# A recurrent block with a routed mixture of experts: x loads first, logits three chunks ahead, routing in smaller steps, dispatches in one row

## What is computed

```python
xn = _layernorm(x)
# s: a gated recurrence along each sequence
hidden, gate = split(xn @ W_hg)            # 256 columns each
a = sigmoid(-gate);  v = sigmoid(gate) * (relu(hidden) + 0.5)
h[t] = a[t] * h[t-1] + v[t];   s = h @ W_out
# ffn: one shared expert, and the best 2 of 16 experts by softmax(xn @ Wr)
shared = silu(xn @ Sg) * (xn @ Su) @ Sd
routed = sum over the 2 experts e:  p_e * (silu(xn @ Wg[e]) * (xn @ Wu[e]) @ Wd[e])
out = x + s * silu(routed + shared)
```

## Time and profile before

| | us |
|---|---|
| median of 3 runs (467.46, 472.47, 469.41) | 469.41 |
| profiled execution, its own time | 466.69 |
| its span (first to last instruction) | 464.5 |
| first phase, to ACT's last copy of it | 216.4 |
| PE idle for the dispatches of group 0 | 216.4 to 246.5 |
| second phase, first `gate_up` to last | 248.64 to 439.08 |
| PE / DVE / ACT / POOL busy | 324.3 / 257.2 / 243.9 / 184.8 |

### The profile page before, as it was taken

How to read it: one execution, slowest core, us unless ns; L and a number is a source line. 1 busy time by engine, 2 the same in 40 slices (tenths; PEclk the granted TensorE clock), 3 DMA queues, 4 the chain that set the end, 5 groups by cost and what they waited for, 6 DMA issues and landing times. The chain is left out here.

```text
span 464.5 us, 6051 instructions
## 1 busy us (share of the span) xinstructions
PE 324.3 (70%) x1532; PEld 206.5 (44%) x1532; DVE 257.2 (55%) x692; ACT 243.9 (53%) x518; POOL 184.8 (40%) x206
## 2 busy tenths in 40 slices
PE   0735999998957878894006644739889899989930
PEld 0423566655634445563003423515555555555520
DVE  3105587887885496797002740616656566666640
ACT  1552787688875447774004421526666566666520
POOL 4803111111111107636650477555445455555571
PEclk9985999999988789998556887779999999999985
DMA  4299999300000003452338135153444444444200
GB/s 142 85 331 418 412 414 377 165 2 1 1 1 0 1 0 133 176 223 100 128 140 276 65 130 206 65 156 102 126 133 138 139 139 137 121 118 119 71 3 0
DMA packets 27982, 63.81 MB, mean 137 GB/s; under 512 B 3701, under 2 KB 22784, under 8 KB 27056
## 3 DMA queue, kind: packets, MB, share of 16 engines
q1 hardware_dynamic: 20880, 45.78, 28.6%
q0 software_dynamic: 6784, 17.06, 9.9%
q10 hardware_dynamic: 288, 0.60, 0.4%
HBM read 29.52 MB, written 35.21 MB: 139 GB/s over the span
## 5 line engine op out<-in xcount | busy, mean ns | idle before, releaser
L318 POOL DMA_INDIRECT out<-arena x84 | 87.2, 1038 | 75.9 <-DVE arena L787 59.5
L899 PE MATMUL p_u<-xT,w_front 128*128 128x512 f32 x192 | 100.3, 659 | 2.1 <-DVE prod L526 2.0
L312 POOL DMA_INDIRECT slots<-arena,pos x64 | 65.6, 1024 | 65.2 <-issue 37.9
L763 DVE TENSOR_TENSOR arena<-p_u,arena 128x512 f32<-128x512 f32 x42 | 29.0, 691 | 109.0 <-ACT arena L423 93.7
L972 PE MATMUL p_u<-arena 128*128 x168 | 84.0, 624 | 0.0
L997 PEld LDWEIGHTS p_s<-arena 128*128 128x128 f32 x336 | 43.1, 198 | 53.7 <-issue 53.7
L997 PE MATMUL p_s<-arena 128*128 x336 | 49.5, 292 | 22.6 <-ACT arena L429 9.1
L409 ACT ACTIVATE arena<-arena 128x128 f32<-128x128 f32 x84 | 36.6, 483 | 51.0 <-DMA arena<-slots 50.8
L899 PEld LDWEIGHTS p_u<-xT,w_front 128*128 128x128 f32 x192 | 37.7, 212 | 37.3 <-issue 37.3
L276 POOL TENSOR_TENSOR var_eps<-meanvar,eps 128x4 f32<-128x4 f32 x16 | 3.5, 221 | 127.4 <-DVE meanvar L492 127.4
L948 PE MATMUL p_xt<-ident,arena 128*128 128x128 f32 x84 | 18.2, 301 | 46.6 <-ACT arena L409 45.3
(11 more groups left out here) (124 smaller groups left out, 468.5 us busy)
## 6 DMA issues: line engine op xcount, KB each, us to landing
slots<-arena SPq DMA_DIRECT2D x4, 4116.0 KB, 19.7
arena<-slots SPq DMA_DIRECT2D x42, 392.0 KB
arena<-in_W_lines SPq DMA_DIRECT2D x2, 2688.0 KB, 12.5
arena<-in_x SPq DMA_DIRECT2D x16, 256.0 KB, 14.4
arena<-in_W_lines SPq DMA_DIRECT2D x1, 2304.0 KB, 9.2
out<-arena POOLq DMA_INDIRECT x84
slots<-arena,pos POOLq DMA_INDIRECT x64
w_front<-in_W_front ACTq DMA_DIRECT2D x1, 392.0 KB, 3.6
```

The costliest lines, as they stand in the source:

```text
L312: pool.indirect_dma_start(slots, index, xrow[:, t], None).then_inc(signal, 16)
L318: pool.indirect_dma_start(out, index, xg[:, n % RX, h, X], None, bounds_check=T - 1, oob_is_err=False)\
L763: nc.vector.tensor_tensor(hg[:, :, :], p_u[:, n % 2 * 2:n % 2 * 2 + 2, 2 * P:4 * P], sil[:, n % 2], ALU.mult)\
L899: nc.tensor.matmul(p_u[:, n % 4], w_front[:, UPS[q]:UPS[q] + P], xT[:, c % XB], start=True, stop=True)\
```

## The change

- **x first.** SP issues all 16 chunks of x, then waits for the blank rows and issues the four fills.
- **Three ahead.** A table `READ` replaces `LEAD`: chunks 1, 2 in round 0; 3 in round 1; 4, 5 in round 2; i + 3 after that. `xT` gets four buffers, the statistics three. On PE the transposes stay between `up` 1 and 2, and the logits go from the middle of the round to its end; chunk 0's go behind its first two `up`. ACT's wait for all constants before the first normalisation is gone.
- **Routing spread.** Keys are made once per group (rounds 8 and 14). Group 0: counts in round 8, bases and first half in 9, second half in 10, probabilities in 9. Group 1: all in rounds 13 to 15. Each step stands at the start of DVE's round, ahead of `ln_stats` and the scans. The weights are split: DVE makes probabilities, POOL multiplies and adds (`block_weights`).
- **Dispatches.** POOL waits per half for positions and per chunk for `s_she`; no wait for its own dispatches; no store between group 1's dispatches.
- **Twelve slot buffers.** `RX` = 12; to make room, `sil`, `hg`, `hw`, `hT` of the second phase move onto the recurrence's buffers, free after the scans.

```diff
-XB = 3
-RX = 8
+XB = 4
+RX = 12
...
+        READ = {0: [1, 2], 1: [3], 2: [4, 5]} | {i: [i + 3] for i in range(3, NCH - 3)}
...
             for c in range(NCH):
                 load_x(c)
-                if c == 3:
-                    sp.wait_ge(s_blank, 2)
-                if c >= 3 and c % 3 == 0 and c < 15:
-                    q = c // 3 - 1
-                    rows = slots[q * SLOTS * P // 4:(q + 1) * SLOTS * P // 4]
-                    sp.dma_start(rows.rearrange("(p n) w -> p (n w)", p=P), arena[:, 0:SLOTS // 4 * ROW]).then_inc(s_init, 16)
+            sp.wait_ge(s_blank, 2)
+            for q in range(4):
+                rows = slots[q * SLOTS * P // 4:(q + 1) * SLOTS * P // 4]
+                sp.dma_start(rows.rearrange("(p n) w -> p (n w)", p=P), arena[:, 0:SLOTS // 4 * ROW]).then_inc(s_init, 16)
...
+            def block_weights(g):
...
+                pool.wait_ge(s_p01, g + 1)
+                weights = p01[:, :, a:b].rearrange("p k (t w) -> p k t w", w=1).to_broadcast([P, 2, n, BLOCK])
+                nc.gpsimd.tensor_tensor(eq4[:, :, 0:n], eq4[:, :, 0:n], weights, ALU.mult).then_inc(s_spot, 1)
+                pool.wait_ge(s_spot, g + 1)
+                nc.gpsimd.tensor_tensor(xrow[:, a:b, W4:W4 + BLOCK], eq4[:, 0, 0:n], eq4[:, 1, 0:n], ALU.add).then_inc(s_w4, 1)
+
+            for c in range(3, NCH):
                 rstd_of(c)
+            block_weights(0)
+            pool.wait_ge(s_w4, 1)
             pool.wait_ge(s_init, 64)
-            pool.wait_ge(s_w4, 1)
-            pool.wait_ge(s_pos, len(HALVES[0]))
-            pool.wait_ge(s_she, CHUNKS[0].stop)
             for t in TILES[0]:
-                if t > 0 and t % 8 == 0:
-                    pool.wait_ge(s_disp[0], 16 * min(t, FIRST_TILES))
-                    if t > FIRST_TILES:
-                        pool.wait_ge(s_disp[1], 16 * (t - FIRST_TILES))
+                if t == HALVES[0][0][0]:
+                    pool.wait_ge(s_pos, 1)
+                if t == HALVES[0][1][0]:
+                    pool.wait_ge(s_pos, 2)
+                if t % TT == 0:
+                    pool.wait_ge(s_she, t // TT + 1)
                 dispatch(s_disp[0] if t < FIRST_TILES else s_disp[1], t)
+            block_weights(1)
             pool.wait_ge(s_w4, 2)
-            pool.wait_ge(s_pos, len(HALVES[0]) + len(HALVES[1]))
-            pool.wait_ge(s_she, NCH)
-            early = [10, 14, 18]
-            for k, t in enumerate(TILES[1]):
-                if k in early:
-                    store_out(early.index(k))
+            pool.wait_ge(s_pos, 3)
+            for t in TILES[1]:
+                if t % TT == 0:
+                    pool.wait_ge(s_she, t // TT + 1)
                 dispatch(s_disp[2], t)
-            for n in range(len(early), PAIRS):
+            for n in range(PAIRS):
                 store_out(n)
...
+                if i == 7:
+                    route_top(2)
                     route_second(2)
                     shift_logits(0)
+                if i == 8:
+                    route_keys(0)
+                    count_keys(0)
+                if i == 9:
+                    key_bases(0)
+                    positions(0, 0)
+                if i == 10:
+                    positions(0, 1)
                 if i == 11:
                     tile_keys(0)
                     route_top(3)
+                if i == 12:
+                    route_second(3)
+                if i == 13:
+                    route_top(4)
                     route_second(4)
                     shift_logits(1)
+                if i == 14:
+                    route_keys(1)
+                    count_keys(1)
+                if i == 15:
+                    key_bases(1)
+                    positions(1, 0)
+                for c in read(i + 2):
+                    ln_stats(c)
+                rec_scan(i, 0)
+                for c in read(i + 1):
+                    ln_bias(c)
+                rec_scan(i, 1)
+                for c in read(i):
+                    copy_logits(c)
+                if i == 9:
+                    probabilities(0)
+                if i == 15:
+                    probabilities(1)
+                    tile_keys(1)
                 shared_gated(i)
...
+                for c in read(i):
+                    logits(c)
+                if i == 8:
+                    prefix(0, 0)
                 if i == 9:
-                    prefix(0, 0)
-                if i == 10:
                     prefix(0, 1)
+                if i == 14:
+                    prefix(1, 0)
```

More of the change, by code:

```diff
@@ L218, in recurrent_moe_block, with read @@
         FIRST_TILES = FREE_CHUNKS * TT
-        def read_ahead(i):
-            return [1, 2] if i == 0 else [i + LEAD] if i + LEAD < NCH else []
+        READ = {0: [1, 2], 1: [3], 2: [4, 5]} | {i: [i + 3] for i in range(3, NCH - 3)}
+        def read(i):
+            return READ.get(i, [])
         @block.sync
@@ L434, in ffn_gate @@
                 nc.scalar.activation(summed, summed, ACT.Silu).then_inc(s_gate, 1)
-            act.wait_ge(s_const, CONSTS)
             normalise(0)
             copy_xT(0)
-            normalise(1)
+            for c in read(0):
+                normalise(c)
             act.wait_ge(s_wfront, 16)
             for i in range(NCH):
-                ahead = read_ahead(i)
                 rec_in(i, 0)
[L444 to L447, removed]
+                for c in read(i):
+                    copy_xT(c)
                 rec_in(i, 1)
@@ L566, in route_second, with route_keys @@
                 first_of(q, lg2[:, 0:b - a], m1, 1)
-            def route_keys(q):
+            def route_keys(g):
                 nonlocal steps
-                a, b = BATCHES[q]
+                a, b = TILES[g].start, TILES[g].stop
                 n = b - a
@@ L787, in out_rows @@
                 nc.vector.tensor_tensor(rows[:, :, X], rows[:, :, X], rows[:, :, SHARED], ALU.add).then_inc(s_o, 1)
[L789 removed]
+            for c in [0] + read(0):
                 ln_stats(c)
                 ln_bias(c)
[L792 removed]
+            for c in read(1):
+                ln_stats(c)
             copy_logits(0)
+            dve.wait_ge(s_const, CONSTS)
             for i in range(NCH):
[L795 to L811 removed]
                 if i == 2:
@@ L888, in up @@
                 pe.wait_ge(s_xTe, c + 1)
+                if n == 0:
+                    pe.wait_ge(s_wfront, 16)
                 if n >= 4:
@@ L1002, in _ @@
             transpose_x(0)
-            logits(0)
             for i in range(NCH):
-                ahead = read_ahead(i)
                 up(i, 0)
                 up(i, 1)
-                if ahead:
-                    transpose_x(ahead[0])
+                if i == 0:
+                    logits(0)
+                for c in read(i)[:1]:
+                    transpose_x(c)
                 up(i, 2)
                 up(i, 3)
+                for c in read(i)[1:]:
+                    transpose_x(c)
                 if i >= 1:
@@ L1014, in _ @@
                     shared_down(i - 1)
-                if ahead:
-                    logits(ahead[0])
                 up(i, 4)
                 up(i, 5)
-                if i == 0:
-                    transpose_x(2)
-                    logits(2)
+                for c in read(i):
+                    logits(c)
+                if i == 8:
+                    prefix(0, 0)
                 if i == 9:
-                    prefix(0, 0)
-                if i == 10:
                     prefix(0, 1)
+                if i == 14:
+                    prefix(1, 0)
             rec_down(NCH - 1)
@@ L1033, in _ @@
                 gate_up(n)
-                if n == 0:
-                    prefix(1, 0)
                 if n + 1 < PAIRS:
```

111 lines of the change are left out of this document (33 added, 78 removed).

## The result

The kernel after takes 410.42 us (median of 4 runs, 407.2 to 411.8), the kernel before 470.94: a ratio of 0.871 (0.863 to 0.879). The forecast was 372, the range 360 to 402. So the sign was right and the time lay outside the range, 38 us above the forecast. The profiled run took 411.8 us, its span is 409.8.

The account below looks back on a forecast made before the run. No engine named as the overall bound; PE or a chain close to it bounds the dense stretches. First `gate_up` 194.1 + pairs 146.0 + cold start 2 + tail 25.4 = 367.5 span, plus 2.2 and 2.7: 372 us, range 360 to 402.

Parts of the forecast that it names:

- No stops: POOL's forty dispatches without the stops' 14.2 us: 52.3 us, last start 185.3, first phase ending beside it at 186.
- Rival B: PE's hold-up beside long dispatch rows comes again in pairs 0 to 8: 372 + 18.4 = 390; chance 0.24.
- A: The main forecast, with every part of the change working as summed: 372 us, own range 360 to 383; chance 0.44.
- x first: Start: PE's 12.28 us and ACT's 2.81 us waits go; round 1's transposes come at 31.
- Logits last: Rounds: logits leave the loop, a round takes 9.4 us instead of 9.99, as PE's own work is 9.38.
- Rival C: Rounds don't get denser, 9.99 us each (+7), and DVE slips as now (+11.4): 391; chance 0.12.
- Round 2: First phase: this round reads two chunks and so takes 1.3 us more.
- Routing: Rounds 7 to 10: DVE's spread routing overloads by 7.1 us, PE's prefix sums add 0.9: 8 us, round 10 at 125.
- First dispatch: POOL: starts at 133 against 174.50, behind round 10's statistics and two new POOL operations of 1.4 us.
- D: DVE's scans hold POOL up 1.22 us more for each of 40 dispatches: 372 + 49 = 421; chance 0.07.
- E: Pairs: loads still wait for stores, 3.98 us for all pairs: 372 + 41 x 0.42 = 389; chance 0.05.
- F: Slower than before: POOL's queue fills and a dispatch takes as long as its transfer, 3 us giving 481; chance 0.05.

Follow-up runs that it names:

- affected chips: Chips where the unchanged kernel before took 468.7, 469.6 or 470.9 us and PE was held up; the kernel after took 410.42 and 411.32 us there.
- quiet chip: Kernel after, unchanged, on a chip without hold-ups, where the kernel before took 462.94 us: 371.52 us, ratio 0.802.
- second run of the kernel after: Kernel after, unchanged, on another chip, where the kernel before took 469.63 us: 411.32 us, ratio 0.877.

## Why the prediction was right and wrong

**The step that failed** is the overlap under *No stops*: "The idle 31 us are covered". The sum of 372 has no term for a hold-up, beside the row of forty or in the pairs, and the two took 20.4 and 19.5 us, measured against the chip without them. Rival B named the mechanism and put it in pairs 0 to 8 alone, at 18.4 us; it was kept out of the first phase by "group 0's rows of eight show nothing of the kind". But the change takes the stops out of the row of forty. Rows of eight in group 0 show no hold-up in three runs on affected chips (stops twice, pauses once), and without stops the kernel before is held up there too. So the same mechanism had to be put beside chunks 12 to 15 as well. B with both, the second size known only now, is 372 + 18.4 + 20 = 410. The evidence was in the earlier trace rows: a hold-up of 18.4 us in a row of POOL's without a stop. A mechanism admitted with a chance of 0.24 has to be applied to every place where the change creates its condition; the range would then have reached 410. The chance was too low as well: what the trace of before showed, on that kind of chip, was to be expected again.

**A, step by step**, where nothing held up. The round starts are those of the result's run, from before its hold-up; the quiet chip's are 0.25 to 0.5 us later. From the last dispatch on, the numbers are the quiet chip's, where 371.5 us were measured:

- *x first*: round 1's transposes at 31.99 (31 forecast; 32.24 quiet).
- *Logits last*: the rounds take 9.16 us (54.22 to 63.38, for 9.4): less than the 9.38 that PE was busy for before, so that was no floor. Rival C fell.
- *Round 2*, with its two chunks, took 13.07 us (41.15 to 54.22): 3.9 more than 9.16, where 1.3 was put.
- *Routing*: round 10 at 124.36 (125). The overload was 6 us and not 8: 14.35 for round 8 (100.03 to 114.38) and 9.98 for round 9. So round 10 was hit by luck in part: 2.2 us too many for the rounds and 2 for the routing stand against 2.6 too few for round 2 and 1 for the start.

```profile
54.22 0.60 PE L870 MATMUL p_xt<-ident,xn 128*128 128x128 f32 x4
63.38 0.60 PE L870 MATMUL p_xt<-ident,xn 128*128 128x128 f32 x4
114.38 0.60 PE L870 MATMUL p_xt<-ident,xn 128*128 128x128 f32 x4
124.36 0.60 PE L870 MATMUL p_xt<-ident,xn 128*128 128x128 f32 x4
```

- *First dispatch*: 134.83 (133). POOL's two new operations took 1.69 + 0.52 = 2.2 instead of 1.4.
- *No stops*: last start at 190.57 where nothing held up (185.3): 55.2 us for the row (from 135.34) instead of 52.3, as its forty dispatches took 1107 ns on the mean, not 1035. That is what came of D: 72 ns a dispatch instead of 1220. Its mechanism is there, though. A dispatch that begins inside a scan of DVE's, with 0.7 us or more of it to come, ends 0.77 us after the scan does and takes 1.5 to 1.8 us instead of 0.96, in six of the seven cases of this row; two of them, from the timelines of POOL and DVE:

```profile
164.40 1.83 POOL L319 DMA_INDIRECT slots<-arena,pos  x1 [0.31 <-issue]
166.53 1.54 POOL L319 DMA_INDIRECT slots<-arena,pos  x1 [0.30 <-issue]
```

```profile
163.59 1.87 DVE L666 TENSOR_TENSOR_SCAN cum<-carry,oh 128x820 bf16<-128x820 bf16 x1
166.08 1.22 DVE L530 TENSOR_TENSOR_SCAN rec<-rec 128x512 f32<-128x512 f32 x1
```

  The prediction said "no such wait was in them" of the forty before, from their mean; two of them, at 211.36 and 214.62, end 0.77 us after a scan in the same way. A mean hides a wait that falls on a few. The Trainium skill, "SBUF — State Buffer", section "SBUF: two separate sides", lets DVE and GpSimd block each other for a whole instruction; these six rows agree with that, the dispatch waiting for the rest of the scan. The seventh, at 156.08, does not: it began 0.04 us behind a scan and took 0.96 us. As a dispatch can wait for the rest of a scan alone, the price stays far below D's.
- *First `gate_up`*: 200.22 (194.1), 9.65 behind the last dispatch instead of 8.8.
- *Group 1*: pair 9 wasn't late (230.60, 30.4 us after pair 0). *Ring*: with 8 buffers PE waits 7.74 us at pair 8 (forecast 8). E fell for twelve. So did F: the row's pace was 1.42 us on the mean, on the quiet chip, where it was slower; far from 2.9.
- *Pairs and tail*: 143.95 and 25.7 (148 and 25.4). The pace of 3.56 holds from pair 6 on; the first ones ran at 3.3.

Sum: span 369.9 for 367.5. So on the quiet chip 372 would have been hit partly by luck: the span was 2.4 too small, and the 2.7 us added for the median were not there (371.7 profiled, 371.52 median). And the rows of the forecast came from an affected chip, where the kernel before took 469: as a ratio to the kernel before 372 is 0.79, the quiet chip gave 0.802 and the affected ones 0.871 and 0.877.

## What to carry to other kernels

A long row of indirect DMAs from POOL is not free for the others: on some chips the engines that wait for PE stood still for up to 30 us beside it, and a break of 1 us at every eighth costs about 4 us in all where it isn't needed and saves 21 where it is. A wait that looks like pure loss can be the break that keeps a neighbour alive; when it is taken out, look at what ran beside it. An unexplained hold-up in a profile is a term of the sum wherever its condition will hold. A difference between two kernels is worth measuring on more than one chip.

## What was not expected of the hardware

- The chips differ: the same program takes 371.5 and 411.3 us, while the kernel's runs on one chip lie within 1.1% (407.2 to 411.8). Whether it is the chip, or something else that differed from set to set, no run tells apart.
- While POOL issues indirect DMAs one after another (0.3 us between two), PE's results reach ACT and DVE up to 26.5 us late on affected chips (30.0 in the second run of the kernel after), from 24 to 32 us into the row of forty (11 in the second row, 9 in the kernel before), at 158 GB/s and at 51. Some of these waits end while the row goes on, others up to 4.4 us after its last dispatch. The Trainium skill, "SBUF — State Buffer", section "SBUF: two separate sides", says that PE and ACT never wait on anyone at the SBUF ports; no run here places the delay, and on affected chips PE does wait. The Trainium skill, "Perfetto Trace Analysis", section "Tensor Engine Instruction (MATMUL, LD_WEIGHTS)", says that a matmul's recorded end is estimated and that its semaphore is raised once PSUM has acknowledged the writes. By that, late acknowledgements and late signals would look alike in these traces, and the 26.5 us between record and signal fit both.
- A dispatch that begins in the midst of a scan of DVE's takes up to 1.83 us instead of 0.96 and ends 0.77 us after the scan, before the change and after it.
- In the standstill the granted clock fell to 0.50 of 2.4 GHz, that is 1.2 GHz, and the first products after it took 2.05 us a pair instead of 1.10.
- What it is in a row of dispatches (the issuing or the number of rows), how long a row an affected chip bears, and what differs between the chips, stays open. Every run here was profiled, so the profiler's own traffic is not ruled out.
